# A graph network with experts in two parts instead of three, the second part's results gathered in the next stage

## The reference

```
x = x + gnn0(layernorm(x))      # two-way graph attention, fused
x = x + experts(layernorm(x))   # each node uses 2 of 8 experts
x = x + gnn1(layernorm(x))      # attention over edges, with q, k, v and skip tables
x = x + slices(layernorm(x))    # attention over slices
```

```
gate = x @ Wg + bg;  the two largest of 8 gates choose a node's experts
h = gelu(x @ W1[e] + b1[e])     # 256 -> 512
y = h @ W2[e] + b2[e]           # 512 -> 256
out = sum of y over the node's two experts
q, k, v, skip = x @ Wq + bq, x @ Wk + bk, x @ Wv + bv, x @ Ws + bs
```

## Time and profile before

| | us |
|---|---|
| median of 3 runs | 6730.26 (6723.53 to 6736.85) |
| profiled execution | 6732.85 |
| its span, first to last instruction | 6731.1 |
| PE busy in it | 3097.8 (46%) |
| DVE busy | 4045.9 (60%) |
| POOL busy | 3282.5 (49%) |
| mean granted TensorE clock | 0.697 of full |

### The profile page before, as it was taken

One profiled execution on the slowest core, in us unless ns is written; L12 is line 12 of the kernel. 1 busy time (PEld: TensorE's weight loads), 2 busy tenths in 40 slices (PEclk: granted clock), 3 DMA queues, 4 the chain that ended last, 5 costly groups with the idle time before them and its releaser, 6 DMA issues. The chain is left out here.

```text
span 6731.1 us, 52372 instructions
## 1 busy us (share of the span) xinstructions
PE 3097.8 (46%) x13150; PEld 2333.9 (35%) x13150; DVE 4045.9 (60%) x7640; ACT 1419.6 (21%) x2477; POOL 3282.5 (49%) x3326
## 2 busy tenths in 40 slices
PE   4612200000000000287888584676666666765677
PEld 3501200000000000145555333555555555654446
DVE  3635667775544444335333355888888888887672
ACT  2012222222333333112222101111111111111220
POOL 0165656777777777522302244555555555553200
PEclk9555555555555555556999797888888888887788
DMA  2122353332353333213322226888888888886113
GB/s 83 42 62 82 91 164 94 97 96 78 107 196 96 103 96 103 84 45 119 98 64 83 64 109 193 250 253 252 248 248 248 249 253 254 253 245 200 58 49 132
DMA packets 292291, 948.99 MB, mean 141 GB/s; under 512 B 84513, under 2 KB 125096, under 8 KB 250597
## 3 DMA queue, kind: packets, MB, share of 16 engines
q0 software_dynamic: 167376, 470.76, 25.4%
q1 hardware_dynamic: 124772, 476.69, 20.6%
HBM read 626.13 MB, written 332.84 MB: 142 GB/s over the span
## 5 line engine op out<-in xcount | busy, mean ns | idle before, releaser
L1274 PE MATMUL e_psE<-e_we,e_eaT 128*128 128x256 f32 x3136 | 977.3, 441 | 605.8 <-ACT e_eaT L1217 529.7
L801 POOL DMA_INDIRECT g_g<-t,rec x784 | 777.3, 991 | 416.0 <-issue 267.9
L1274 PEld LDWEIGHTS e_psE<-e_we,e_eaT 128*128 128x128 f32 x3136 | 695.1, 226 | 750.9 <-ACT e_eaT L1217 552.7
L801 POOL DMA_INDIRECT g_g<-t,dst_of x784 | 789.1, 1007 | 291.9 <-issue 291.9
L1140 POOL DMA_INDIRECT e_kv<-kv,rec x784 | 772.5, 985 | 245.4 <-issue 245.4
L1133 POOL DMA_INDIRECT e_q<-q,q_of x392 | 380.8, 971 | 699.4 <-DVE e_at L1174 582.3
L1432 PE MATMUL j_psM<-ident,tail 128*128 128x128 f32 x32 | 7.1, 413 | 1217.4 <-PEq L53 1217.4
L1275 PE MATMUL e_psE<-e_kv,ident 128*128 128x256 f32 x1568 | 530.0, 423 | 0.0
L838 DVE TENSOR_TENSOR_SCAN g_wv<-g_fx,g_wv 128x2176 f32<-128x2176 f32 x98 | 458.9, 4683 | 0.2 <-issue 0.2
L1170 DVE TENSOR_TENSOR e_q<-e_psE,e_q 128x512 f32<-128x512 f32 x392 | 269.5, 688 | 270.9 <-DMA state_b<-j_new,j_rowto 230.2
L1432 PEld LDWEIGHTS j_psM<-ident,tail 128*128 128x128 f32 x32 | 6.7, 319 | 1218.2 <-issue 1218.2
(11 more groups left out here) (512 smaller groups left out, 6579.2 us busy)
## 6 DMA issues: line engine op xcount, KB each, us to landing
state<-e_st SPq DMA_DIRECT2D x98, 1088.0 KB
e_ea<-in_edge_attr SPq DMA_DIRECT2D x98, 896.0 KB
state_f<-g_st SPq DMA_DIRECT2D x49, 1088.0 KB
state_b<-g_st SPq DMA_DIRECT2D x49, 1088.0 KB
m_work<-xs SPq DMA_DIRECT2D x119, 128.0 KB
ys<-m_work SPq DMA_DIRECT2D x119, 128.0 KB
xs<-g_ta SPq DMA_DIRECT2D x28, 512.0 KB
g_g<-t,rec POOLq DMA_INDIRECT x784
```

The lines of the kernel that those rows point to most:

```text
L801: pool.indirect_dma_start(g[:, u, j, :], None, tab, bass.IndirectOffsetOnAxis(ap=at_, axis=0)).then_inc(gat[u], 16)
L1274: nc.tensor.matmul(half, eaT[:, m, j, k, :], we[:, k, :], start=(k == 0), stop=False)
```

## The change

`PARTS` becomes (2, 5): 35 and 77 tiles, 112 in all. Two columns per tile are placed in the loop instead of one. The second part's results are not gathered and added in `experts`. In `layer1_tables`, POOL gathers them group by group into a new ring of two groups (`collect`: 14 transfers), for groups 2 and 3 at the stage's start, for groups 4, 5, 6 behind the q scatters of groups 0, 1, 2; DVE adds them in `receive`, ahead of the group's normalization. `slot` moves from the stage to the kernel's lasting buffers. DVE's loop over groups is written out instead of looping over pairs.

```
-PARTS = (2, 3, 2)
+PARTS = (2, 5)
...
-            for n in range(len(PARTS)):            # POOL, gathers of experts
+            for n in range(len(PARTS) - 1):
...
-                if t < NI - first_col[1]:
-                    place(first_col[1] + t)
+                for i in range(first_col[1] + 2 * t, min(NI, first_col[1] + 2 * t + 2)):
+                    place(i)
...
-            for i in range(first_col[-2], NI):
-                finish(i)
...
+        FIRST, RING = PARTS[0], 2
+        got = sb("got", [P, RING, GT, 2, D])
+        landed = [sem("landed0"), sem("landed1")]
+        added = sem("added")
...
+            def collect(g):                         # POOL
+                if g >= FIRST + RING:
+                    pool.wait_ge(added, g - FIRST - RING + 1)
+                c.alone(pool)
+                for j in range(GT):
+                    for k in range(2):
+                        pool.indirect_dma_start(got[:, g % RING, j, k, :], None, c.ys[1], bass.IndirectOffsetOnAxis(
+                            ap=c.slot[:, g * GT + j, k:k + 1], axis=0)).then_inc(landed[g % RING], 16)
+
+            for g in range(FIRST, FIRST + RING):
+                collect(g)
             pool.wait_ge(slots_made, 1)
             for g in range(NG):
                 pool.wait_ge(rows, g + 1)
...
+                if FIRST + RING + g < NG:
+                    collect(FIRST + RING + g)
                 if g:
                     pool.wait_ge(sc[1 - g % 2], 2 * GT * 16 * ((g - 1) // 2 + 1))
                     pool.sem_inc(q_free, 1)
...
+            def receive(g):                         # DVE
+                r = g % RING
+                xg = c.x[:, g * (GT * D):(g + 1) * (GT * D)].rearrange("p (j d) -> p j d", d=D)
+                v.wait_ge(landed[r], 2 * GT * 16 * ((g - FIRST) // RING + 1))
+                tt(xg, got[:, r, :, 0, :], xg, ALU.add)
+                v.drain()
+                tt(xg, got[:, r, :, 1, :], xg, ALU.add).then_inc(added, 1)
+                v.drain()
+
             def prepare(g, par):
+                if g >= FIRST:
+                    receive(g)
                 normalize_group(c, v, w, xln, g, vin, root, xr)
...
-            over_groups(v, prepare, step)
+            prepare(0, 0)
+            for g in range(NG):
+                step(g, g % 2, g + 1 < NG)
```

More of the change, by code:

```diff
@@ L2720, in build @@
         c.tail = sb("tail", [P, SW])
+        c.slot = sb("slot", [P, NI, 2], I32)
         c.flag, c.lastkey = sb("flag", [P, 1], I32), sb("lastkey", [P, 2], I32)
```

4 lines of the change are left out of this document (2 added, 2 removed).

## The result

The changed kernel took 6744.24 us (median of 12 runs, 6737.98 to 6764.23), the kernel before on the same chip 6725.65 us (12 runs, 6710.07 to 6745.81). The ratio is 1.003, 95% interval 1.0019 to 1.004: slower by 0.3%. I had predicted 6702 us, faster.

A forecast was written before the change was run, and what follows sets the result against it. The prediction took TensorE to bound the expert loop at 5.19 us a tile and group boundaries to matter in the layer-1 stage. Its terms, -78.6 + 2 + 12.6 + 34.4 + 1 = -28.6 us, gave 6702 us, range 6684 to 6724.

The forecast's parts named there:

- (a): Expert loop: seven tiles fewer at 5.19 us, 36.3 us off; second place per tile taken as 0, bounds 0 to +7.
- Rival 3: Expert loop waits for scatters because the ring of four columns lands too late; 6747 us at 15.4 us latency; chance 0.04.
- (b): After the expert loop: the tail of gathers and adds goes, 37.5 us off.
- (c): Ahead of the expert loop: one slots fewer, so the loop starts about 4.8 us earlier.
- (d): Layer-1 stage's start: 28 gathers share queues with weights and start, +2 us (bounds 0 and 4); their POOL time hidden.
- (e): Layer-1 groups: receive's two VectorE adds cost 4.2 us in each of steps 1, 4 and 5, 12.6 us in all.
- (g): Layer-1 steps 2 and 3: TensorE's clock after the long stands, 0 to +6 us, taken as +1; written-out loop taken as 0.
- (f): Layer-1 steps 2 and 3: VectorE waits for q_free's increment behind 14 gathers, +17.2 us per step, +34.4 us in all.
- the lock: Layer-1 groups: receive's adds hold POOL's second and third scatter, 2.0 us in all per step, bounds 0 and 4.
- Rival 2: Layer-1 stage: TensorE's clock stays at 1.2 GHz for the group after each long stand, +24 us, 6725 us; chance 0.10.
- theory L: Formed during the experiments: past some 16 to 26 us of POOL's unbroken indirect-DMA stream, VectorE and ScalarE stand until it ends.

The follow-up runs named there:

- a1: The changed kernel itself, run on a quicker chip: 6227.91 us against 6258.1 for the kernel before, ratio 0.9951.
- d1: The changed kernel once more, on a third quicker chip: 6230.24 us against 6260.38 for the kernel before, ratio 0.9953.
- a2: The kernel before, unchanged, profiled on the same quicker chip as a1: one run, 6262.11 us.
- b2: Changed kernel, slower chip: q_free increment ahead of the gathers, second column only every sixth tile, opening gathers held until the first tile's products: 6754.44 us, ratio 0.9981.
- b1: Changed kernel, slower chip: q_free increment ahead of the gathers, VectorE's steps 1 to 4 as a loop again: 6787.78 us, ratio 1.003.
- a3: Changed kernel, quicker chip, without the layer-1 stage's 70 gathers (ring set to zero once and still added): one run, 6203.76 us.
- e3: Kernel before, quicker chip, with only VectorE's layer-1 loop over groups written out: 6254.8 us, ratio 0.999.
- b4: Kernel before with VectorE's layer-1 loop written out, the same code as e3, on a slower chip: one run, 6783.58 us.
- e1: Changed kernel, quicker chip, with POOL's q_free increment put ahead of the 14 gathers of a collect: 6201.49 us against 6259.11, ratio 0.9904.
- c5: Kernel before, slower chip, each layer-1 group's 14 scatters followed by 14 more into an unused table, no gathers: one run, 6824.24 us.
- c6: Changed kernel, slower chip, with POOL's order in a group made q_free increment, gathers, then scatters: one run, 6742.76 us.
- c2: Changed kernel, slower chip: early q_free increment, second column every sixth tile, POOL waiting for its last burst to land before more gathers: 6670.87 us, ratio 0.9921.
- e4: Changed kernel, quicker chip, placing one column per tile and a second only every sixth tile: 6227.14 us, ratio 0.9944.

## Why the prediction was wrong

On two quicker chips the change gives -30.2 and -30.1 us (a1, d1), and I had summed -28.6. That it comes so near is luck in part: between the profiles of a1 and a2 the stretches that the change touches give -42 us (5.6 before the loop, 38.0 in it and 43.9 behind it off, 45.2 in the stage on), and the stages behind, in which nothing differs, give 10 back. On the chip of the first comparison it gives +18.6. So the steps go one by one:

- **(a), the step that failed first: "I take 0" for the second `place` per tile.** On the slower chip the loop shrank by 19.3 us instead of 36.3; b2 against b1 puts 25 us on the second column. I had checked that POOL's 5.04 us fit into 5.19 and priced VectorE's work and the landing (0 to +7). That POOL's stream becomes nearly unbroken, and that TensorE, which is the loop's bound, is late beside it (increments up to 5.5 us behind the matmuls), was in none of my bounds. On the quicker chip the 0 held: 611.2 to 573.2 is -38.0. Rival 3 had this place and another mechanism (the ring's slots); line 1867 shows no such wait.
- **(b)** came out larger: -43.9 instead of -37.5, as the next stage starts 2.8 us after the last add and not 6.6. **(c)** was right: -4.9 against -4.8.
- **(d), the step that failed second: "I take +2" for the stage's start.** It was +17.0 on the slower chip, and +4.0 or +2.4 on the quicker ones. I had called the 28 gathers' 35 us of POOL "hidden", as POOL's own work is; the stands of VectorE and ScalarE beside the stream, for TensorE's late transposes, are not.
- **(e)** The two adds take 2.02 us each, but a group with `receive` takes 6.9 us more than one without (37.5 against 30.6), not 4.2, because the clock falls each time behind TensorE's longer gap: 8 matmuls take 6.37 us behind gaps of 7.8 to 7.9 us in a3, and 3.70 behind those of groups 1 to 3 in e3. That I said under (g) that the clock falls in the present gap anyway was right for the kernel before; the written-out loop, which I had taken as nothing, would have saved some 3 us in most groups (30.6 us in three of e3's and three of b4's). The two errors cancel: 37.5 against the 34 of before is +3.5, for which I had +4.2.
- **(f)** was right in kind and size. The increment comes 22.7 us after the group's first scatter (3882.4 - 3859.72; 5.7 + 17.5 = 23.2 predicted), the first eviction 23.6 us after the scale's end (24.0 predicted, 26.0 with the lock; the lock's 1.7 us are there, but the sequencer ran twelve transfers ahead and not ten, 2.5 us earlier), and without the wait groups 2 and 3 take 21.9 us less on the quicker chip (e1 against a1), where 34.4 less the 8.4 of the two receives, 26, were predicted. The lock is there, as the 1.83 and 1.78 us of the second and third scatter show. The Trainium skill ("SBUF — State Buffer", Who interferes with whom) has a GpSimd instruction that reads SBUF stand for a two-input VectorE instruction's whole length; the trace agrees in kind. Its depth of 8 for GpSimdE's queue ("TensorE: Matmul & The Clock Gate") does not fit: at 3882.4 two of the 14 gathers had begun, so the sequencer was twelve ahead.
- **(g)** was right: behind the long stands 8 matmuls take 5.83 us, no more than the 6.56 of the earlier trace rows, and the tile behind them is not slow. Rival 2 falls. One further tile in each of groups 1 to 3 is slow (5.26, 6.69 and 5.40 us by its rows), behind TensorE's gap at the stand.
- **What the sum left out: the stands inside groups 1 to 3.** Net of the `q_free` wait they cost 10.1, 7.9 and 7.8 us there (47.7, 56.8 and 55.5 us against 37.6, 48.9 and 47.7 in a1), together 26. With 17 in the loop and 15 at the start that is 58 us. Less the 6.4 of (b) and the 6.2 by which the rest of the stage came out under my sum it is 45, and with the 3.9 of the stages ahead 49, which is what lies between my -28.6 and the +20.8 of the two spans; by the medians (+18.6) it is 47.

That TensorE is late beside POOL's long streams in these two stages is shown: c5 brings the stands into the kernel before with scatters alone, c6 keeps them in place with the contents exchanged, c2 removes most of them with pauses of 2.3 us, and e4's edit (in b2) removes them from the loop. Why a stream does it is not shown. One candidate was the loading of instructions. The Trainium skill ("Runtime: NRT & Kernel Launch", Instruction fetch mechanics) says that each engine's instructions are fetched in blocks over a DMA queue of its own, and that this is mostly hidden. The traces speak against held-up blocks, as far as they list them: VectorE and ScalarE wait for a semaphore and not for code, the matmuls whose increments are late had begun, and from 3824 to 3941 us of the changed kernel, where the increments of 3849.50, 3853.78 and 3901.24 fall, the DMA view has no packet of the two instruction queues, which carried 46 and 94 over the span. No run tells why some chips show the stands and others none. Nor did I run the pauses beside the changed kernel on one slower chip.

The kernel before had a trace of it that I did not read: its longest waits list 643 us of ScalarE in the edge pass behind the layer-1 tables with an unnamed releaser. On the quicker chip that row is gone, and the 328 us that stand there are put down to TensorE.

```profile
ACT e_eaT L1217 <- remote: 643.1, 107, 7.8
```

```profile
ACT e_eaT L1217 <- PE e_psT L1264: 328.4, 86, 17.0
```

The two kernels before are the same, and 470 us apart. The semaphores say that TensorE is the releaser in both: on the slower chip 99 of the 104 longer waits of line 1217 (over 1.5 us) end with an increment of TensorE that comes over 1 us after its transposes' rows, 6.1 us in the median; on the quicker chip (a2) none of 79 does, and the median is 0.01 us.

These rows also bound what theory L may say. One turn of the edge pass, POOL and VectorE:

```profile
5010.41 0.94 POOL L1133 DMA_INDIRECT e_q<-q,q_of  x1 [7.53 <-DVE e_at L1174]
...
5024.52 0.95 POOL L1140 DMA_INDIRECT e_kv<-kv,rec  x1 [0.30 <-issue]
5031.93 0.94 POOL L1133 DMA_INDIRECT e_q<-q,q_of  x1 [6.46 <-DVE e_at L1174]
```

```profile
5027.48 0.69 DVE L1170 TENSOR_TENSOR e_q<-e_psE,e_q 128x512 f32<-128x512 f32 x1 [2.73 <-DMA state_b<-j_new,j_rowto]
```

POOL's bursts are of 12 gathers and 15 us here, with pauses of 6.5 to 7.5 us, and still the increment that ends this wait comes at 5027.45, at least 8.8 us after its product's row (the last one before ends at 5018.65) and 2.0 us after the burst. So the length of the stream isn't all that counts. What else does is open; 8 of the 12 gathers bring rows of 512 numbers and not 256, and no run varied that.

## What to carry to other kernels

An engine that only issues DMAs can cost the others time without any shared buffer or semaphore: before POOL's work is called hidden, look beside its streams of indirect DMAs for increments of TensorE that come later than its rows. Where they did here, breaking the stream helped: bursts of 14 (18 us) with pauses of 2.3 us, with the other edits of c2, gave 0.9921. It is no general bound, as the edge pass is late with shorter bursts and longer pauses. An increment that another engine waits for belongs ahead of such a burst: moving `q_free`'s gave 24 us on the quicker chips, and no gain in the time (b1) where TensorE was late anyway. A wait whose releaser is unnamed or impossible is a reading of its own: look up the semaphore, who raises it in this stage and when the record has its increment. And a change worth under 1% should be timed on more than one chip: this one is 0.3% slower on one and 0.5% faster on two.

## What was unexpected of the hardware

- With POOL issuing indirect DMAs 1.25 to 1.27 us apart without a gap, increments of TensorE came up to 18 us (b2) after the rows of their matmuls, on the slower chips alone. VectorE and ScalarE waited for them, from 16 to 32 us after the stream's first DMA until -3 to +4 us about its last, for 9 to 19 us at a time in the layer-1 stage.
- One and the same kernel took 6726 to 6769 us on some chips and 6258 to 6260 us on three others.
- Behind gaps of 3.57 to 3.65 us in TensorE's work the clock stayed up in some groups (8 matmuls 3.70 us) and fell in others (5.11 to 6.38 us); behind 7.8 to 7.9 us it fell each time (6.35 to 6.38 us).
- POOL's sequencer ran twelve indirect DMAs ahead of its engine.
